# Gather, weights, second layer norm and attention prologue of a two-layer transformer in one stage

## What is computed

```
x   = x + gate_moe * (cw * results[slot of the token])     # layer 0, the experts' answers gathered by token
m   = mean(x); v = var(x)
h   = (x - m) / sqrt(v + 1e-5) * scale + shift             # the norm ahead of the attention (ln2)
q,k = rope(h @ Wq.T), rope(h @ Wk.T);  v = h @ Wv.T        # 16 heads of 8
p   = softmax(causal(q @ k.T) * 8 ** -0.5)
x   = x + gate_attn * ((p @ v) @ Wo.T)
```

## Time and profile before

| | |
|---|---|
| median of 3 runs | 2022.4 us (2019.75 to 2032.22) |
| the profiled execution | 2020.08 us |
| its span in the trace | 2018.4 us |
| PE busy | 1609.6 us, 80% |
| DVE busy | 1350.4 us, 67% |
| ACT busy | 1008.6 us, 50% |
| POOL busy | 995.3 us, 49% |
| ln2 stage in the trace, first to last instruction | 1153.4 to 1228.7 us |
| attention stage from its first instruction to its first score matmul | 1229.0 to 1298.8 us |

### The profile page before, as it was taken

The page is one execution under the profiler, slowest core; times in us unless marked ns, Lnnn a source line. Parts: engine busy times, 40 slices in busy tenths (PEclk is TensorE's granted clock), DMA queues, the critical chain, the costliest instruction groups (busy, mean ns, idle before and its releaser), DMA issues. The chain is left out here.

```text
span 2018.4 us, 23347 instructions
## 1 busy us (share of the span) xinstructions
PE 1609.6 (80%) x7291; PEld 726.9 (36%) x7291; DVE 1350.4 (67%) x1529; ACT 1008.6 (50%) x1641; POOL 995.3 (49%) x524
## 2 busy tenths in 40 slices
PE   7778878778878877865919646788898889879998
PEld 5222222222222222211717533354454444633333
DVE  3089999999999999997522113566666564384444
ACT  3577776777777777762304223144444455451121
POOL 1179999999999999997251253011111100050000
PEclk8988999998998898878859856599998889989999
DMA  3143444333344444431033212332222330100001
GB/s 143 29 112 96 102 105 103 95 100 96 99 105 105 105 105 105 101 100 37 5 89 91 74 37 68 93 80 61 55 67 63 81 81 3 47 1 0 0 0 42
DMA packets 78636, 145.41 MB, mean 72 GB/s; under 512 B 10214, under 2 KB 40782, under 8 KB 76854
## 3 DMA queue, kind: packets, MB, share of 16 engines
q1 hardware_dynamic: 75350, 134.98, 25.8%
q0 software_dynamic: 3216, 9.51, 1.4%
HBM read 87.27 MB, written 23.53 MB: 55 GB/s over the span
## 5 line engine op out<-in xcount | busy, mean ns | idle before, releaser
L614 POOL TENSOR_TENSOR PR<-H,CS 128x1024 f32<-128x1024 f32 x256 | 598.3, 2364 | 40.5 <-DVE H L590 20.6
L590 DVE TENSOR_TENSOR_SCAN H<-DA,X 128x1024 f32<-128x1024 f32 x192 | 431.0, 2272 | 0.0
L484 PE MATMUL psY<-PR,fold 128*64 128x512 f32 x1024 | 295.7, 672 | 6.3 <-POOL PR L614 6.3
L578 DVE TENSOR_TENSOR X<-DU,psB 128x1024 f32<-128x1024 f32 x192 | 235.7, 1228 | 58.6 <-DMA DU<-ab 36.4
L1322 ACT ACTIVATE a_PT<-a_psS 128x512 f32<-128x512 f32 x320 | 181.3, 601 | 156.8 <-PE a_psS L1226 153.1
L1369 DVE TENSOR_REDUCE a_MX<-a_psM 128x1 f32<-128x384 f32 (+3 forms) x352 | 206.4, 635 | 72.7 <-PE a_psM L1241 71.5
L566 ACT ACTIVATE DA<-DT,negA 128x511 f32<-128x511 f32 x384 | 249.5, 710 | 1.1
L1240 PE MATMUL a_psM<-a_kst,a_qst 72*128 72x512 bf16 (+3 forms) x512 | 148.8, 338 | 25.1 <-DMA a_kst<-scratch_k 14.4
L1225 PE MATMUL a_psS<-a_qst,a_kst 75*128 75x512 bf16 (+3 forms) x512 | 141.3, 324 | 16.5 <-DMA a_qst<-m_scratch 15.3
L625 POOL TENSOR_TENSOR XS<-DU,BS 128x1024 f32<-128x1024 f32 x64 | 150.9, 2358 | 0.0
L590 DVE TENSOR_TENSOR_SCAN H<-X,XS 128x1024 f32<-128x1024 f32 x64 | 146.1, 2283 | 3.7 <-POOL XS L625 3.4
(11 more groups left out here) (268 smaller groups left out, 2689.7 us busy)
## 6 DMA issues: line engine op xcount, KB each, us to landing
CS<-c_rows SPq DMA_DIRECT2D x128, 256.0 KB, 4.0
DT<-W SPq DMA_DIRECT2D x64, 256.0 KB, 4.3
DU<-ab SPq DMA_DIRECT2D x64, 256.0 KB, 4.0
BS<-c_rows SPq DMA_DIRECT2D x64, 256.0 KB, 4.3
scratch_q<-a_partsq SPq DMA_DIRECT2D x24, 384.0 KB, 3.3
a_qst<-scratch_q SPq DMA_DIRECT2D x8, 1152.0 KB
a_kst<-scratch_k SPq DMA_DIRECT2D x24, 384.0 KB
scratch_k<-a_partsk SPq DMA_DIRECT2D x8, 384.0 KB, 4.6
```

The source lines that it names most:

```text
L484: last = nc.tensor.matmul(psY[h * HP:(h + 1) * HP, n % 2 * T:(n % 2 + 1) * T], fold[:, :], chunk(PR[n % 4], h), start=False, stop=n >= NS - 2)
L578: nc.vector.tensor_tensor(both(X[s % 2][:, :]), DU[p][:, at:at + 2, :], psB[:, :].unsqueeze(1).to_broadcast([P, 2, T]), ALU.mult).then_inc ...
L590: nc.vector.tensor_tensor_scan(H[s % 4][:, :], decay, x, 0.0, ALU.mult, ALU.add).then_inc(scan_done, 1)
L614: nc.gpsimd.tensor_tensor(both(PR[s % 4][:, :]), both(H[s % 4][:, :]), CS[q % 2][:, s // 2 % 2, :].unsqueeze(1).to_broadcast([P, 2, T]), A ...
```

## The change

The ln2 stage and the class `Combine` go; gather, weights, residual and norm are written into the attention stage, with the operations unchanged in kind and shape. Four things differ from a plain joining of the two stages. First, batch 0 goes alone through gather, weights, norm and projections; the rounds of batches 1 to 7 (`pe_lead`, `act_lead`, `dve_lead`, skewed as before) lie at written places between projections, rope steps, maxima A and maxima B. Second, POOL issues 16 gathers at the start and the other 16 in twos between the rope steps of batch 0 and in a run of eight after the clearing of `VA`. Third, the PSUM buffers of the norm are one of each kind (the score banks `psS` and the value bank `psO`), and `gtok` and `sq` lie in the buffers `PT`, with the weights multiplied in place. Fourth, the two counters `act_init` and `hb_ready` become one, `act_copy`. `act_lead(n)` has weights n, square n-1, deviation n-2, shift n-4; `dve_lead(n)` has residual n, centered n-1, reciprocal n-2, scale n-3, each leaving out batch 0.

```diff
...
-class Combine:
...
+def attention_stage(nc, W, W3, pack3, tiles, scratch_q, scratch_k, m_scratch, hT, xT, identb, gate, results, cw, gather_at, moe_gate, scale, shift):
...
-        PT = [[sb(f"PT{i}{u}", [P, T]) for u in range(5)] for i in range(4)]
+        PTS = sb("PT", [P, 20, T])
+        PT = [[PTS[:, 5 * i + u, :] for u in range(5)] for i in range(4)]
+        gtok = PTS[:, 10:18, :].rearrange("p b (k d) -> p (b k) d", d=P)
+        sq = [PTS[:, 18 + i, :] for i in range(2)]
+        sd, rs = sb("sd", [P, NT]), sb("rs", [P, NT])
...
-        def pool_rope(pool, b, x, used):
+        def pool_rope(pool, b, x, step, used):
             q = parts[x]
-            pool.wait_ge(mb_used, used)
-            if x or not isinstance(b, int) or b > 0:
-                pool.wait_ge(part_step, 4 * b + 2 * x)
-            nc.gpsimd.tensor_tensor(QR[:, :], TA[:, :], TB[:, :], ALU.add).then_inc(rope_step, 1)
-            pool.wait_ge(part_step, 4 * b + 2 * x + 1)
-            nc.gpsimd.tensor_tensor(R[:, :], QR[:, :], q[:, 0, :], ALU.subtract).then_inc(rope_step, 1)
-            pool.wait_ge(part_step, 4 * b + 2 * x + 2)
-            nc.gpsimd.tensor_tensor(q[:, 2, :], R[:, :], q[:, 1, :], ALU.subtract).then_inc(rope_step, 1)
+            if step == 0:
+                pool.wait_ge(mb_used, used)
+                if x or b > 0:
+                    pool.wait_ge(part_step, 4 * b + 2 * x)
+                nc.gpsimd.tensor_tensor(QR[:, :], TA[:, :], TB[:, :], ALU.add).then_inc(rope_step, 1)
+            elif step == 1:
+                pool.wait_ge(part_step, 4 * b + 2 * x + 1)
+                nc.gpsimd.tensor_tensor(R[:, :], QR[:, :], q[:, 0, :], ALU.subtract).then_inc(rope_step, 1)
+            else:
+                pool.wait_ge(part_step, 4 * b + 2 * x + 2)
+                nc.gpsimd.tensor_tensor(q[:, 2, :], R[:, :], q[:, 1, :], ALU.subtract).then_inc(rope_step, 1)
...
+        def pe_tokens(pe, b):
+            pe.wait_ge(weighted_ready, 4 * b + 4)
+            if b >= 1:
+                pe.wait_ge(x_ready, b)
+            for k in range(4):
+                last = nc.tensor.transpose(psS[0][:, k * P:(k + 1) * P], gtok[:, 4 * b + k, :], ident)
+            last.then_inc(gps_ready, 1)
+        def pe_center(pe, b):
+            pe.wait_ge(x_ready, b + 1)
+            if b >= 1:
+                pe.wait_ge(copied, b)
+            nc.tensor.matmul(psS[1][:, :], center, tile(xT, b), start=True, stop=True).then_inc(xc_ready, 1)
+        def pe_variance(pe, b):
+            pe.wait_ge(sq_ready, b + 1)
+            if b >= 1:
+                pe.wait_ge(sd_ready, b)
+            for k in range(4):
+                last = nc.tensor.matmul(psO[:, k:k + 1], sq[b % 2][:, k * P:(k + 1) * P], mean, start=True, stop=True)
+            last.then_inc(var_ready, 1)
+        def pe_rows(pe, b):
+            pe.wait_ge(rs_ready, b + 1)
+            if b >= 1:
+                pe.wait_ge(scaled, b)
+            for k in range(4):
+                at = 4 * b + k
+                last = nc.tensor.matmul(psS[2][:, k * P:(k + 1) * P], rs[:, at:at + 1].to_broadcast([P, P]), ident, start=True, stop=True)
+            last.then_inc(rb_ready, 1)
+        def act_weights(act, b):
+            act.wait_ge(gathered[b], 64)
+            for at in range(4 * b, 4 * b + 4):
+                nc.scalar.activation(gtok[:, at, :], gtok[:, at, :], ACT.Copy, scale=cw[:, at:at + 1]).then_inc(weighted_ready, 1)
...
+        def pool_gather(pool, first, last):
+            for at in range(first, last):
+                nc.gpsimd.indirect_dma_start(gtok[:, at, :], None, results, bass.IndirectOffsetOnAxis(ap=gather_at[:, at:at + 1], axis=0)
+                                             ).then_inc(gathered[at // 4], 16)
+        def pe_lead(pe, n):
+            if n < B:
+                pe_tokens(pe, n)
+            if 1 <= n - 1 < B:
+                pe_center(pe, n - 1)
+            if 1 <= n - 2 < B:
+                pe_variance(pe, n - 2)
+            if 1 <= n - 3 < B:
+                pe_rows(pe, n - 3)
...
+                sp.dma_start(W3[:, :], pack3).then_inc(fetched, 16)
...
-                pe.wait_ge(act_init, 2)
-                for n, (b, name) in enumerate([(b, name) for b in range(2) for name in PRO]):
-                    pe_use(pe, name, n or None, b, 0)
-                pe.wait_ge(hb_ready, 1)
+                pe_tokens(pe, 0)
+                pe_center(pe, 0)
+                pe_variance(pe, 0)
+                pe_rows(pe, 0)
+                pe_tokens(pe, 1)
+                pe.wait_ge(fetched, 16)
+                pe.wait_ge(h_ready, 1)
+                for n, name in enumerate(PRO):
+                    pe_use(pe, name, n or None, 0, 0)
+                for n in range(2, 6):
+                    pe_lead(pe, n)
+                pe.wait_ge(h_ready, 2)
+                for n, name in enumerate(PRO):
+                    pe_use(pe, name, n + 4, 1, 0)
+                pe.wait_ge(act_copy, 3)
                 pe_use(pe, "V", 8, 0, 0)
+                for n in range(6, B):
+                    pe_lead(pe, n)
                 pe.sem_inc(PV_done, 1)
                 pe.wait_ge(st_loaded[0], LOADS)
                 pe_maxima(pe, 0, 0, 0, 0, NG)
                 pe.wait_ge(m_step, 5)
                 pe_use(pe, "MA", 9, 0, 0)
+                for n in range(B, B + 3):
+                    pe_lead(pe, n)
                 pe_maxima(pe, NG, 0, 1, 0, NG)
                 pe.wait_ge(m_step, 10)
                 pe_use(pe, "MB", 10, 0, 0)
                 pe.wait_ge(m_loaded[0], 16)
                 pe.wait_ge(ones_loaded, 32)
+                pe.wait_ge(h_ready, B)
                 for k in range(2):
                     for u in range(5):
                         pe_scores(pe, 0, 0, k, u)
@@ -1514,12 +1614,27 @@
 
             @block.scalar
             def _(act):
-                nc.scalar.copy(mqk[:, :], w("mask_qk")).then_inc(act_init, 1)
-                nc.scalar.copy(mkq[:, :], w("mask_kq")).then_inc(act_init, 1)
-                nc.scalar.copy(HB[:, :], hT[:, 0:T]).then_inc(hb_ready, 1)
-                for b in range(2):
-                    for step in range(4):
-                        act_part(act, b, step)
+                act_weights(act, 0)
+                act_square(act, 0)
+                act_deviation(act, 0)
+                act_shift(act, 0)
+                act_weights(act, 1)
+                act.wait_ge(fetched, 16)
+                nc.scalar.copy(mqk[:, :], w("mask_qk")).then_inc(act_copy, 1)
+                nc.scalar.copy(mkq[:, :], w("mask_kq")).then_inc(act_copy, 1)
+                act.wait_ge(h_ready, 1)
+                nc.scalar.copy(HB[:, :], hT[:, 0:T]).then_inc(act_copy, 1)
+                act_lead(act, 2)
+                act_part(act, 0, 0)
+                act_lead(act, 3)
+                for step in range(1, 4):
+                    act_part(act, 0, step)
+                for n in range(4, B):
+                    act_lead(act, n)
+                for step in range(4):
+                    act_part(act, 1, step)
+                for n in range(B, B + 4):
+                    act_lead(act, n)
                 act.sem_inc(O_copied, 1)
                 for k in range(2):
                     act_exps(act, 0, k)
@@ -1528,31 +1643,57 @@
             @block.vector
             def _(dve):
                 nc.vector.memset(ones3[:, :], 1.0).then_inc(ones_ready, 1)
-                for n, (b, name) in enumerate([(b, name) for b in range(2) for name in PRO]):
-                    dve_use(dve, name, n, -1, b, 0)
+                dve_residual(dve, 0)
+                dve_centered(dve, 0)
+                dve_reciprocal(dve, 0)
+                dve_scale(dve, 0)
+                dve_residual(dve, 1)
+                for n, name in enumerate(PRO):
+                    dve_use(dve, name, n, -1, 0, 0)
+                for n in range(2, 6):
+                    dve_lead(dve, n)
+                for n, name in enumerate(PRO):
+                    dve_use(dve, name, n + 4, -1, 1, 0)
                 dve.wait_ge(pool_init, 3)
                 dve_use(dve, "V", 8, -1, 0, 0)
+                for n in range(6, B):
+                    dve_lead(dve, n)
                 dve_maxima(dve, 0, 0, 0, 0, NG)
                 dve_use(dve, "MA", 9, -1, 0, 0)
+                for n in range(B, B + 3):
+                    dve_lead(dve, n)
                 dve_maxima(dve, NG, 0, 1, 0, NG)
                 dve_use(dve, "MB", 10, -1, 0, 0)
                 turns(dve, lambda c: dve_turn(dve, c))
 
             @block.gpsimd
             def _(pool):
+                pool_gather(pool, 0, 16)
+                pool_rope(pool, 0, 0, 0, 2)
+                pool_gather(pool, 16, 18)
+                pool_rope(pool, 0, 0, 1, 2)
+                pool_gather(pool, 18, 20)
+                pool_rope(pool, 0, 0, 2, 2)
+                pool_rope(pool, 0, 1, 0, 4)
+                pool_gather(pool, 20, 22)
+                pool_rope(pool, 0, 1, 1, 4)
```

(43 more changed lines are left out.)

69 lines of the change are left out of this document (35 added, 34 removed).

## The result

The changed kernel took 2012.4 us (median of 20 runs) where the kernel before took 2026.0 on the same chip: a ratio of 0.9938, 95% interval 0.9918 to 0.9957. The profiled execution took 2009.7 us, its span 2008.0. So the number of the forecast, 2010, held.

The account below looks back on a forecast made before the run. No engine was full: a chain of short operations bound the stage, with 17 us of unexplained stall. The summed chain put the first score 9.4 us earlier; 3 for the clock made 12.4, giving 2010 us, 8-in-10 range 1997 to 2028.

Parts of the forecast that it names:

- (a): Start of the new stretch: the first four gathers are issued as before, 7.5 us.
- (b): Batch 0 alone through weights, residual and norm, with handoffs, up to its first projection: 15.2 us.
- (c): Projections of batch 0, with the rope of q waiting for all of it behind square 1 on ACT: 14.8 us.
- (d): Rope of batch 0 on ACT and POOL, with round 3 and gathers between its steps: 16.1 us.
- (e): Norm rounds 4 and 5 with PE full, 6.45 us each at the low clock: 12.9 us.
- (f): Projections of batch 1, four at 2.86 us each at the low clock: 11.4 us.
- (g): V, 2.1 us, and norm rounds 6 and 7, 12.9 us, at the low clock.
- (h): Maxima A: 14.8 us from first matmul to DVE's last step, and about 0.7 for MA.
- (i): Norm rounds 8 to 10, between maxima A and maxima B: 12.0 us.
- the clock comes up: Rival: PE gets the high clock through full stretches from round 4 on; gain 9.4 + 18, time 1995; chance 0.20.
- Stall stays or grows: Rival: PE, ACT and DVE handoffs stall beside POOL's gathers; 17 us gives 2027, 35 us gives 2045; chance 0.18.
- The rival on failing cover: Rival: batch 0's load or a stalled rope makes PE wait before maxima A; 2014 to 2022 us; chance 0.08.

Follow-up runs that it names:

- e4: The kernel before, no edit, run again for a second trace; fetch to first score 131.6 us.
- e8: The kernel before, no edit, run a third time for its trace; fetch to first score 127.7 us.
- e11: The kernel before, no edit, run once more for a fourth trace; fetch to first score 131.3 us.
- e3: The kernel before, with POOL waiting ahead of its 17th and 25th gathers; 2027.7 us, ratio 1.0066 to the kernel before.
- e5: The changed kernel again, no edit; 2016.3 us against 2015.4 for the kernel before, ratio 1.0010.
- e1: The changed kernel's single stage in the old order, all rounds and 32 gathers before the projections; 2017.45 us, ratio 1.0011 to the kernel before.
- e2: The changed kernel with all 32 gathers issued first, ahead of batch 0's rope; 2019.7 us, ratio 1.0035 to the kernel before.
- e6: The changed kernel with only ACT's order changed, rope casts and weights moved ahead; 2006.6 us, ratio 0.9947 to the kernel before.
- e7: e6 with 24 gathers first and the last eight behind batch 0's rope; 2003.1 us, ratio 0.9935 to the kernel before.
- e9: The changed kernel with five added matmuls in TensorE's pauses at the attention's end; 2014.3 us, ratio 1.0006 to the kernel before.
- e10: e7 with five added matmuls in TensorE's pauses at the attention's end; 1999.9 us, ratio 0.9936 to the kernel before.
- e12: e7 with SP's two transfers of the rows of ones held until batch 0's norm is done; 2003.2 us, ratio 0.9939 to the kernel before.

## Why the prediction came out right, and where it was wrong

One table of the traces, in us. "Start" is SP's fetch of the pack; the attention runs from the first score to the start of the last residual, the tail from there to the end of the span.

| trace | start | to first score | attention | tail |
|---|---|---|---|---|
| before | 1153.4 | 145.4 | 430.0 | 289.6 |
| before: e4, e8, e11 | 1162.8, 1158.2, 1156.7 | 131.6, 127.7, 131.3 | 430.9, 430.7, 431.1 | 289.7, 289.6, 296.5 |
| e3 | 1161.1 | 139.6 | 432.0 | 289.6 |
| after | 1152.7 | 128.4 | 430.2 | 296.8 |
| after: e5 | 1160.1 | 127.7 | 430.0 | 296.7 |
| e1 | 1154.0 | 130.6 | 424.0 | 296.6 |
| e2 | 1160.7 | 131.3 | 430.0 | 293.5 |
| e6 | 1160.1 | 120.7 | 430.4 | 296.5 |
| e7 | 1157.3 | 115.9 | 432.6 | 296.6 |
| e9, e10 | 1155.4, 1156.6 | 125.3, 115.1 | 430.2, 430.4 | 295.8, 299.0 |
| e12 | 1157.8 | 118.4 | 429.3 | 296.7 |

**The stall, the step that decided.** I took 17 us of stall in the old kernel as a property of it and 0 in the new one, and wrote that without the stall the new order would be the slower by some 8 us. Both halves failed. The size was about right: the stretch of the first trace is 13.8 to 17.7 us longer than in e4, e8 and e11. But the stall is in one of five traces of the old order (e3's, with its paced gathers, among them). The kernel before had a median of 2026.0 us on the first chip, and 2014.6, 2015.4, 2014.7 and 2015.9 on the four others; the changed one 2012.4 and then 2016.3. That fits a stall which the old kernel met on the first chip and not elsewhere.

The two first traces show more of this, in a stage that the change leaves alone. The earlier trace rows is a DVE instruction of the route stage that stands 0.54 us behind the one before it, beside POOL's scatters. The changed kernel's first trace has such waits too, up to 1.19 us:
```profile
1024.26 0.22 DVE L911 TENSOR_REDUCE rank<-pos 128x8 f32<-128x64 f32 x1 [1.19 <-DVE pos L910]
1026.38 0.17 DVE L918 TENSOR_TENSOR send<-send,W 128x8 f32<-128x8 f32 x1 [0.85 <-DVE send L917]
```
and e4, like each of the other eleven traces from the four other chips, has none over 0.13 us there:
```profile
1028.84 0.17 DVE L917 TENSOR_TENSOR send<-send,ok 128x8 f32<-128x8 f32 x1
1029.04 0.17 DVE L918 TENSOR_TENSOR send<-send,W 128x8 f32<-128x8 f32 x1
```
Waits of DVE for itself of more than 0.3 us sum to 5.8 us there in the first trace of before and to 6.0 in that of after. So the late semaphores belong to the first chip or its session, not to single executions and not to the old kernel alone; what the new kernel was spared is the large form of them beside the gathers. Extra traffic is not the cause as far as the traces tell: in the 46 us from the fetch the first trace moves the same 3.18 MB in the same number of packets as e4's.

What stays open is why the new order had no remote wait on that chip: by its paced gathers, as I had assumed, or by chance. e1, e2 and e3 were meant to tell and ran where the stall does not occur, and there is one trace of each kernel from the first chip. The measured 13.6 us of the first comparison are therefore mostly an escape from the stall, and that the order gives this escape is argued and not shown.

**The order itself,** without a stall: 127.7 to 131.6 us before (three traces), 125.3 to 128.4 after (the first trace, e5 and e9), some 3 us in its favour by the means, where I had 8 against it (5 with the 3 booked for the clock). The mis-sized terms, by the changed kernel's trace:
- (a) first weights after 10.4 us, not 7.5. SP's two transfers of ones are now issued ahead of that landing, and e12 shows that they cost 2.5 us; in the old kernel they were issued at 1229.68, long behind it. I had left them out.
- (b) as booked within 1 us: 16.1 from the first weights to the first projection (1179.12), 15.2 in my sum.
- (c) and (d): 14.8 + 16.1 = 30.9 booked, 29.2 measured (1179.12 to 1208.31). The size was right, but I took for fixed what was a choice of order on ACT: e6 wins 7.0 of it by moving instructions.
- (e) rounds 4 and 5: 11.0 for 12.9; (f) batch 1's projections: 8.5 for 11.4, 1.91 apart at the high level; (g) V and rounds 6 and 7: 11.5 for 15.0, although ACT stood 9.3 us for the gathers of weights 6. They ran beside load 0: the last of the four was issued by 1218.7 and the weights began at 1228.5, where the first four gathers of the old kernel needed 1.9 us from there. PE had V to do and did not wait for them. Together 8.3 us below the booking, where I had set 3 against it for the clock. The clock rose at 1217.7 while PE had been full since 1208.3, and stayed up through the projections to 1228, which the earlier trace rows had not shown. The Trainium skill ("TensorE: Matmul & The Clock Gate", "What's actually happening") says that the default state is throttled and activity releases it; the trace agrees, some 9 us after PE became full.
- (h) 14.7 for 15.5, (i) 11.7 for 12.0, (j) 15.3 for 15.5. The waits for the load are gone, as booked. Of the two transfers of maxima A, booked at 10 us, the first alone took 15.1 us until the second could be issued, right behind load 1 (5.5 in the old trace), and that hid.

So the step of the sum that failed is the clock's. I had taken 3 us for it; (e), (f) and (g) came out 8.3 us short. First score 1281.0, against 1289.4 forecast. By my own sign, "a clock near 1.0 from 1215", the rival "the clock comes up" came in good part:
```profile
1160.00:1245.00 85.00, 52.24 (x199) 32.16 (x200) 26.62 (x44) 23.76 (x60) 41.25 (x41) 0.64 0.28 69
1215.00:1245.00 30.00, 22.49 (x121) 14.34 (x120) 15.64 (x27) 8.15 (x20) 11.46 (x11) 0.90 0.47 103
```

**What was given back.** I wrote that everything behind keeps its length. The first score is 17.8 us earlier in the first pair of traces, the end only 10.4: the tail is 296.8 us instead of 289.6. It has the same instructions. Windows 0 to 20 and 80 to 100 us behind the last residual, before:
```profile
1728.76:1748.76 20.00, 18.34 (x116) 14.20 (x117) 10.79 (x20) 9.53 (x19) 0.00 (x0) 1.00 0.31 117
1808.76:1828.76 20.00, 16.49 (x55) 6.64 (x56) 6.83 (x11) 4.24 (x8) 0.00 (x0) 0.67 0.01 1
```
and after:
```profile
1711.20:1731.20 20.00, 18.27 (x93) 12.91 (x92) 9.02 (x17) 7.76 (x15) 0.00 (x0) 0.83 0.31 118
1791.20:1811.20 20.00, 12.41 (x43) 4.93 (x43) 8.06 (x15) 4.25 (x8) 0.00 (x0) 0.50 0.00 1
```
DVE and PE do the same work, 213 and 768 instructions from there to the end in both; the clock differs. Over the 288.7 us behind the residual it is granted at 0.94 before and 0.92 after, and PE is busy 263.7 us for 267.3. I first took that for a property of the new kernel, since five traces of it had the long tail and four of the old order the short one (e2 lay between). e11 refutes it as a property of the new kernel alone: there the kernel before has 296.5, with nearly the same windows as the changed kernel.
```profile
1719.10:1739.10 20.00, 18.37 (x93) 13.12 (x94) 9.09 (x17) 7.76 (x15) 0.00 (x0) 0.83 0.32 117
1799.10:1819.10 20.00, 12.75 (x43) 4.93 (x43) 7.85 (x14) 4.25 (x8) 0.00 (x0) 0.50 0.00 1
```
The tail thus has one of a few lengths. The old order got the short one in four of five traces, the new stage in none of nine. That is too lopsided to be put down to luck lightly, but the nine are variants of one another. Whether the chance is different, and what sets it, stays open. It is the likeliest reason why e5 is level with the kernel before although its stretch is some 3 us shorter, but e5 alone can't show it. The attention is not free of this either: it is 6 us shorter in e1, whose profiled execution, 2006.8 us, is the fastest of its twelve.

**How the number came out.** It held by luck, in two ways. The comparison was made on the one chip where the old kernel has the stall; on that of e5 there was no gain to forecast, 2016.3 against 2015.4. And in the first pair of traces two errors stand against each other: the stretch was 17.0 us shorter where I had 12.4, and the tail, which I had at nothing, took 7.2 back.

**The rivals.** "Clock comes up" came for 8.3 of its 18.8 us. "Stall stays or grows" did not come: no trace with the joined stage has a remote wait, though only one of the nine is from the chip where it could. The rival on failing cover is out too: the stack was there when the first maxima wanted it. The rival that I did not have is the plainest: that the stall in the trace of before belongs to where it was taken and not to the kernel.

## What to carry to other kernels

A wait that the order of the code doesn't explain should not be booked as a gain until a second trace of the same kernel, from another chip, shows it again; here it was 17 us of a forecast of 12. An experiment on such a wait has to run where the wait occurs: look for its mark in a part that the change leaves alone. When a chain of short operations is woven into another chain, the gain lies in the in-order list of the engine that serves both: write down for each instruction what it waits for and who is queued behind it, and put the ready one first (7.0 us of the stretch from some ten lines on ACT, 4.8 more on POOL). Then look at what is late next before shortening an early step: 2.5 us won at the first gathers ended in front of POOL's queue.

## What the runs showed of the hardware

- On one chip, waits of DVE for its own last instruction of up to 1.19 us beside indirect scatters, in both traces from it, and in one of them waits of DVE and ACT for a semaphore whose releaser had ended, 19.4 us in sum, beside indirect gathers. In twelve traces from four other chips neither.
- Four traces of the same kernel give a stage start between 1153.4 and 1162.8 us. Spans of single traces don't compare here; stretches between two marks do, to 4 us where there is no stall.
- Two transfers of short rows, 1.76 us of issue, put off the landing of the first indirect gathers by 2.5 us (e7 to e12).
- Four indirect gathers beside the load of batch 0 reached their reader some 10 us after the last was issued, for 1.9 us at the stage's start, and ACT stood 9.3 us for them. The write of maxima A, 24 KB, took 15.1 us from its issue to that of its reading back, right behind load 1, and the same write of maxima B 1.4.
- The clock of TensorE fell 1.1 us behind the last residual in one execution of the kernel before and 28 us behind it in three others, at the same instructions, and the 290 us behind were 7 us longer. Five matmuls in the pauses there kept it up on the spot in e9 and gave no gain that could be measured.
